# Decoder layer, feed-forward part: the quantiser works on centred values, and the deviation moves into the output scale

## What is computed

```
def layer_norm(x):                      # EPS = 1e-6, Q_B = 128
    return (x - mean(x)) / sqrt(var(x) + EPS)
def absmax_quant(x):
    gamma = max(abs(x)); return clip(x * Q_B / gamma, -Q_B + EPS, Q_B - EPS) * gamma / Q_B
def bitlinear(x, w):
    return absmax_quant(layer_norm(x)) @ ternary(w).T * mean(abs(w))
h = gelu(bitlinear(layernorm(x), w_fc))        # 512 -> 2048, per row of x
x = x + bitlinear(h, w_proj)                   # 2048 -> 512
```

## Time and profile before

| | us |
|---|---|
| median of 3 runs (1135.46 to 1136.88) | 1136.7 |
| the profiled execution | 1134.52 |
| its span, first to last instruction | 1132.7 |

### The profile page before, as it was taken

How to read it: one execution, slowest core, us unless ns; L and a number is a source line. 1 busy time by engine, 2 the same in 40 slices (tenths; PEclk the granted TensorE clock), 3 DMA queues, 4 the chain that set the end, 5 groups by cost and what they waited for, 6 DMA issues and landing times. The chain is left out here.

```text
span 1132.7 us, 18945 instructions
## 1 busy us (share of the span) xinstructions
PE 1003.6 (89%) x6034; PEld 760.6 (67%) x6034; DVE 958.9 (85%) x1351; ACT 793.3 (70%) x1529; POOL 625.1 (55%) x509
## 2 busy tenths in 40 slices
PE   7998988999988999789899985887888998989997
PEld 5555666669664668556567664676767776878886
DVE  5758898996998869998986789899999999998654
ACT  4656756765786776888767696827988978984432
POOL 1369485554536796456738831569655655544401
PEclk9999999999988999899999986997899999989999
DMA  5325356364435545323555460420111110000000
GB/s 194 114 76 171 109 151 184 105 198 152 116 103 182 154 131 168 103 81 106 167 190 159 139 194 6 175 105 26 41 47 34 38 33 32 26 16 19 10 19 19
DMA packets 59360, 115.91 MB, mean 102 GB/s; under 512 B 8880, under 2 KB 13232, under 8 KB 58240
## 3 DMA queue, kind: packets, MB, share of 16 engines
q1 hardware_dynamic: 59264, 114.70, 32.4%
HBM read 90.42 MB, written 24.25 MB: 101 GB/s over the span
## 5 line engine op out<-in xcount | busy, mean ns | idle before, releaser
L1248 POOL TENSOR_TENSOR hb<-du,b_bc 128x1024 f32<-128x1024 f32 (+1 forms) x160 | 314.8, 1987 | 160.6 <-PE ps L1708 160.6
L1795 DVE TENSOR_TENSOR_SCAN hb<-ps,hb 128x1024 f32<-128x1024 f32 (+1 forms) x128 | 257.4, 2013 | 33.3 <-ACT ps L1377 20.0
L1377 ACT ACTIVATE ps<-delta,a_neg 128x511 f32<-128x511 f32 (+2 forms) x320 | 180.6, 600 | 79.5 <-DVE hb L1795 73.3
L1817 DVE SCALAR_TENSOR_TENSOR y_acc<-ps,ct,y_acc 128x512 f32<-128x512 f32 x256 | 181.2, 740 | 24.5 <-PE ps L1708 23.8
L1708 PE MATMUL ps<-ident,hb 128*128 128x128 f32 x1088 | 160.1, 288 | 43.8 <-DVE hb L1795 12.7
L1708 PEld LDWEIGHTS ps<-ident,hb 128*128 128x128 f32 x1088 | 127.8, 147 | 72.1 <-issue 14.2
L1487 ACT ACTIVATE p_q<-ps,m_col 128x512 f32<-128x512 f32 (+3 forms) x256 | 131.5, 530 | 20.9 <-DVE m_col L1892 12.2
L1639 PE MATMUL ps<-xn_t,w_ring 128*128 128x512 f32 x256 | 117.9, 604 | 0.8 <-DVE o_t L1908 0.6
L1766 PE MATMUL ps<-t_fc,xq_hi 128*128 128x512 f32 x256 | 106.2, 415 | 3.2 <-DVE hq_lo L2007 3.2
L1682 PE MATMUL ps<-ident,p_q 128*128 128x128 f32 x640 | 91.9, 287 | 14.4 <-ACT p_q L1487 7.2
L1503 ACT ACTIVATE p_t<-ps 128x512 f32<-128x512 f32 x160 | 88.2, 605 | 22.9 <-PE ps L1682 22.6
(11 more groups left out here) (151 smaller groups left out, 2016.5 us busy)
## 6 DMA issues: line engine op xcount, KB each, us to landing
w_ring<-in_w_attn SPq DMA_DIRECT2D x32, 512.0 KB, 3.7
qk_d<-hl SPq DMA_DIRECT2D x64, 256.0 KB
q_st<-qk_d SPq DMA_DIRECT2D x128, 128.0 KB, 2.8
b_bc<-bc_d SPq DMA_DIRECT2D x48, 256.0 KB, 3.9
k_st<-qk_d SPq DMA_DIRECT2D x64, 128.0 KB, 2.7
k_st<-qk_d SPq DMA_DIRECT2D x128, 64.0 KB, 2.3
x_in<-in_x SPq DMA_DIRECT2D x16, 256.0 KB, 2.9
raw_fc<-in_w_fc SPq DMA_DIRECT2D x4, 1024.0 KB, 9.2
```

The costliest lines, as they stand in the source:

```text
L1248: nc.gpsimd.tensor_tensor(piece_of(e, hi, lo).rearrange("p (a n) -> p a n", a=2), du[b % 2][:, 2 * h:2 * h + 2, lo:hi], b_bc[:, i % BC_RIN ...
L1377: ins = nc.scalar.activation(factors(j, hi, lo)[:, (hi - lo) * m + start:(hi - lo) * (m + 1)], delta[b % 2][:, et, lo + start:hi], ACT.Exp ...
L1795: v.tensor_tensor_scan(h, d, h, 0.0, ALU.mult, ALU.add).then_inc(scan_done, 1)
L1817: v.scalar_tensor_tensor(out=y, in0=bank(kind, r, tb), scalar=ct[:, b % 2, tb, n:n + 1], in1=y, op0=ALU.mult, op1=ALU.add).then_inc(y_free ...
```

## The change

Both quantisers now work on the centred row, without the division by the deviation. In xc, DVE subtracts the mean only. In hn, ACT computes mean - h (scale -1 as a constant, bias the mean), and the minus sign is put right in the output scale. The 1/deviation that POOL computes goes into the scale: for xc it is multiplied in beside the weights' mean, for hscale it is made ahead, with the minus sign, by hstat's last instruction. The number of instructions and their shapes stay; the DVE's xc no longer waits for POOL's xa, and ACT's hn no longer for POOL's hstat, but POOL's own scale steps do. Since the 4 slots of the small buffers could now be overwritten early, DVE's BN_AGGR waits for POOL's work on the tile four before. The due times stay as they are.

```
@@ follows
     elif kind == "xc":
-        yield "dve", 1.9, [pool("xa", t), pe("xt", t - 2) if t >= 2 else dve("wo", B - 1, 1, 1)]
-        yield "pool", 1.5, [dve(*item), dve("wtot", 0)] + ([act("fc", t - 4, 3)] if t >= 4 else [])
+        yield "dve", 1.9, [dve("xa", t), pe("xt", t - 2) if t >= 2 else dve("wo", B - 1, 1, 1)]
+        yield "pool", 1.5, [dve(*item), pool("xa", t), dve("wtot", 0)] + ([act("fc", t - 4, 3)] if t >= 4 else [])
...
     elif kind == "hstat":
-        yield "dve", 0.35, [dve("fc", *a, 3)]
-        yield "pool", 1.1, [dve(*item)]
+        yield "dve", 0.35, [dve("fc", *a, 3)] + ([pool("hstat", a[0] - 4)] if a[0] >= 4 else [])
+        yield "pool", 1.1, [dve(*item), dve("wtot", 1)]
     elif kind == "hn":
-        yield "act", 1.3, [pool("hstat", a[0])]
+        yield "act", 1.3, [dve("hstat", a[0])]
...
     elif kind == "hscale":
-        yield "pool", 0.3, [dve(*item), dve("wtot", 1)]
+        yield "pool", 0.3, [dve(*item), pool("hstat", *a)]
@@ POOL, xc
-                    nc.gpsimd.tensor_scalar(f[:, 12:13], f[:, 8:9], gam[:, 0:1], None, ALU.mult).then_inc(fx_scale, 1)
+                    pool.wait_ge(fx_gain, t + 1)
+                    nc.gpsimd.tensor_scalar(f[:, 12:13], f[:, 8:9], f[:, 7:8], gam[:, 0:1], ALU.mult, ALU.mult).then_inc(fx_scale, 1)
@@ POOL, hstat
-                    nc.gpsimd.tensor_scalar(f[:, 3:4], f[:, 0:1], f[:, 2:3], -1.0, ALU.mult, ALU.mult).then_inc(fh_nmr, 1)
+                    pool.wait_ge(gam_ready, 2)
+                    nc.gpsimd.tensor_scalar(f[:, 3:4], f[:, 2:3], gam[:, 1:2], -1.0, ALU.mult, ALU.mult).then_inc(fh_gain, 1)
@@ POOL, hscale
-                    pool.wait_ge(gam_ready, 2)
-                    nc.gpsimd.tensor_scalar(f[:, 12:13], f[:, 8:9], gam[:, 1:2], None, ALU.mult).then_inc(fh_scale, 1)
+                    pool.wait_ge(fh_gain, t + 1)
+                    nc.gpsimd.tensor_scalar(f[:, 12:13], f[:, 8:9], f[:, 3:4], None, ALU.mult).then_inc(fh_scale, 1)
@@ ACT, hn
-                    act.wait_ge(fh_nmr, t + 1)
+                    act.wait_ge(fh_var, t + 1)
-                    nc.scalar.activation(half, half, ACT.Identity, bias=fh[:, t % 4, 3:4],
-                                         scale=fh[:, t % 4, 2:3]).then_inc(hn_done, 1)
+                    nc.scalar.activation(half, half, ACT.Identity, bias=fh[:, t % 4, 0:1], scale=-1.0).then_inc(hn_done, 1)
@@ DVE, xa and xc
+                    if t >= 4:
+                        dve.wait_ge(fx_gain, t - 3)
                     v.bn_aggr(f[:, 0:2], st_x[:, t % 2]).then_inc(fx_var, 1)
...
-                    dve.wait_ge(fx_pow, t + 1)
...
+                    dve.wait_ge(fx_var, t + 1)
-                    own.done(v.tensor_scalar(x, x2(t), f[:, 0:1], f[:, 7:8], ALU.subtract, ALU.mult))
+                    own.done(v.tensor_scalar(x, x2(t), f[:, 0:1], None, ALU.subtract))
@@ DVE, hstat
+                    if t >= 4:
+                        dve.wait_ge(fh_gain, t - 3)
                     v.bn_aggr(f[:, 0:2], st_h[:, t % 2]).then_inc(fh_var, 1)
```

More of the change, by code:

```diff
@@ L973, in layer_kernel @@
         fx_var = sem("fx_var")
-        fx_pow = sem("fx_pow")
+        fx_gain = sem("fx_gain")
         fx_max = sem("fx_max")
@@ L985, in layer_kernel @@
         fh_scale = sem("fh_scale")
-        fh_nmr = sem("fh_nmr")
+        fh_gain = sem("fh_gain")
         hn_done = sem("hn_done")
@@ L1318, in _ @@
                     own.settle()
-                    nc.gpsimd.tensor_scalar(f[:, 7:8], f[:, 2:3], f[:, 3:4], None, ALU.mult).then_inc(fx_pow, 1)
+                    nc.gpsimd.tensor_scalar(f[:, 7:8], f[:, 2:3], f[:, 3:4], None, ALU.mult).then_inc(fx_gain, 1)
                 elif kind == "xc":
```

## The result

| | before | after |
|---|---|---|
| median of the runs, us | 1136.43 (6 runs, 1135.26 to 1136.88) | 1140.39 (6 runs, 1138.35 to 1140.84) |
| ratio, 95% interval | 1 | 1.0033 (1.002 to 1.0046) |
| profiled execution, us | 1134.52, span 1132.7 | 1140.38, span 1138.5 |
| scan 96 starts at, us | 730.99 | 734.68 |
| from scan 96 to SyncE's closing drain, us | 401.5 | 403.6 |

The time lies in the range (1129.5 to 1140.5) but on the other side of before, where rival B had put it. The last two rows serve all that follows. Scan n is the n-th of the 160 pieces into which DVE's scan is cut, and the feed-forward tiles run beside scans 96 to 159; SyncE's closing drain stands 0.2 us ahead of the end of the span. Up to scan 96 every kernel here runs the same instructions in the same order, yet that part ended between 729.6 and 736.5 us from one profiled execution to another.

The account below looks back on a forecast made before the run. DVE was taken to set the pace up to tile 9's quantiser, PE behind it; -2.93 + 1.0 - 0.66 - 0.2 + 1.85 - 0.55 - 1.35 = -2.84 gave 1133.9 us against the median 1136.7, range 1129.5 to 1140.5.

Parts of the forecast that it names:

- rival B: Second block behind the transposes makes gelu late; DVE waits up to 1.86 us at tiles 6 to 9: 1140.3 us; chance 0.24.
- the first of the three pieces of the forecast: Time of tile 9's quantiser; the others are PE's work behind it and what PE waits after that.
- DVE's waits taken away, -2.93: Up to tile 9's quantiser, DVE's waits of 0.93, 0.55 and 1.45 us go: -2.93 us.
- rival A: No change: DVE is full, waits removed before 1007 are made elsewhere, new ones the full 2.9 us: 1135.8 us; chance 0.23.
- New waits, +1.0, with 2.9 as the upper end: On DVE the new order brings its own waits, between none and all removed (0 to 2.9 us): +1.0 us.
- -0.66 for tile 8's output: In DVE's queue the output of tile 8 now stands behind tile 9's quantiser: -0.66 us.
- Pointer, -0.2: DVE's xc reads one scalar per partition less, 0 to 0.8 us over 13 tiles: -0.2 us.
- ACT's pass to 1150: ACT's normalising pass loses a scale operand from memory and goes from 1236 to about 1150 ns.
- Table loads, 0: Three more ACT table loads at 1283 ns put 0 on the path; without cover 3.85 us.
- PE's deferred block, +1.85: On PE, tile 10's second block now stands behind tile 9's transposes, with no later gap to absorb it: +1.85 us.
- Fillers, -0.55: In the full PE stretch, five fillers ahead of tile 13's transposes go: -0.55 us.
- Last chain, -1.35: Near the end, tile 14's chain loses POOL's step, so PE's wait for its quantised row shortens: -1.35 us.

Follow-up runs that it names:

- The run with tile 10's block ahead: Changed kernel with tile 10's second feed-forward block ahead of tile 9's transposes again, on PE and for ACT's gelu: 1139.69 us, ratio 1.0014 to before.
- the clean pair: Changed kernel with tile 10's second block moved ahead of tile 9's transposes, and the same with tile 11's ahead of tile 10's too: 1139.69 and 1135.28 us.
- the run with the dependency from tile 2 on: Changed kernel's instructions, with the planner seeing the shortened dependency only from tile 2 on: 1133.44 us, ratio 0.9979 to before.
- The joined run without them: Changed instructions, new and old order joined at a scan, which one unstated; new first, joined at 120, 128, 144, 152: 1129.55, 1130.67, 1135.73, 1133.59 us.
- POOL's item: Changed kernel with POOL's gain chain of tile 10 back behind its inputs to scans 144 and 145: 1137.85 us, ratio 1.0012 to before.
- the order joined at scan 128: Changed kernel's instructions, in its new order up to scan 128 and the order of before behind it: 1130.67 us, ratio 0.9956 to before.
- the run with 0.59: Changed kernel with tile 11's second feed-forward block ahead of tile 10's transposes again: 1137.37 us, ratio 0.9998 to before.
- the run with the gate additions moved: Changed kernel with two gate additions put ahead of tile 5's third-block statistics and tile 8's search on DVE: 1137.10 us, ratio 0.9999 to before.

## Why the prediction was wrong

Almost all of the miss lies ahead of tile 9's quantiser, the first of the three pieces of the forecast. From scan 96 to its start (the TENSOR_SCALAR on h_sb) it is 275.96 us before, 275.33 with the edit alone (the changed instructions in the order of before) and 278.18 in the changed kernel: 2.2 later, where the sum had it 2.8 earlier (-2.93 + 1.0 - 0.66 - 0.2). Behind it the changed kernel takes 0.2 us less than before, and the sum had 0.05 less (+1.85 - 0.55 - 1.35). By its own steps:

- *DVE's waits taken away, -2.93.* The wait of 0.55 went: tile 9's quantiser is 0.6 us earlier there. The wait of 0.93 at 819.96 did not go (1.42 in that run). It had never been POOL's. ACT's rows of before show what the chain of one row back had hidden:

```profile
816.81 1.28 ACT L1546 ACT_TABLE_LOAD   x1
818.11 0.69 ACT L1546 ACTIVATE h_sb<-ps,fx 128x512 f32<-128x512 f32 x1
818.69 1.23 ACT L1565 ACTIVATE h_sb<-h_sb,fh 128x1024 f32<-128x1024 f32 x1
```

  The pass begins the moment that the gelu ahead of it in ACT's own list lets it: no [idle <-POOL]. And the 1.45 for the projection, which I counted as gone because the output was put elsewhere, became 2.78. In all, DVE's waits up to tile 9's quantiser (those over 0.15 us) are 6.7 us before and 8.1 with the edit alone, while its work there fell by 1.8 us: it came to the others' products sooner. So the argument against rival A, that the same order can only wait less, doesn't hold for DVE.
- *New waits, +1.0, with 2.9 as the upper end.* **This step failed.** DVE's waits up to tile 9's quantiser are 10.3 us in the changed kernel, 3.5 more than before, where I had 1.9 less (-2.93 + 1.0). And the new order, which was to bring that quantiser 1.1 us forward (-1.45 for the projection's wait, -0.66 for tile 8's output, +1.0), puts it 2.85 us back (278.18 for 275.33). I bounded new waits by those removed, and nothing ties the one to the other. The largest has a second price that I left out, the clock after the idle time. Behind the handover it goes on: to tile 11's quantiser DVE spends 315.65 us on 466 instructions, as many as before in 313.09, and the changed ones in the order of before take 309.99. So the new order costs 5.7 us up to there, 2.85 to tile 9's quantiser, 1.0 to tile 10's and 1.8 to tile 11's, and the last is the deferred block below.
- *-0.66 for tile 8's output* is inside the 2.85 us and can't be told apart.
- *Pointer, -0.2.* xc went from 639 to 505 ns with the order of before, 1.6 us in twelve, yet scan 152 came at the same time (+0.03): nothing on the path up to there. The 214 against 154 of the earlier trace rows was too little to go by.
- *ACT's pass to 1150.* 1141 ns. Right.
- *Table loads, 0.* Ninety-nine for ninety-six. A load is 1.28 us and the next activation starts 1.30 us after it began (816.81, 818.11 above). The Trainium skill's "ScalarE: Activation LUTs", section "What ACT_TABLE_LOAD costs", would have it 2.66; no such drain shows here. But the sign that I named for the loads did come. They stand in the chain that ended last, for 20.2 us behind scan 96 (17.4 in before's), five of them between 925.5 and 937.8, ahead of tile 6's first search for the maximum, where before's chain has PE and POOL:

```profile
927.56 1.28 ACT L1360
...
929.75 1.28 ACT L1548
```

  The run with tile 10's block ahead has two loads fewer and gains nothing by it. No run takes the loads away at tiles 6 to 8 alone, so that they cost nothing isn't shown; they are a rival for the part of the loss that has no name.
- *PE's deferred block, +1.85.* 1.7 by the clean pair, and 1.7 again for the run with the dependency from tile 2 on (-2.0 for -3.7). I gave it to tile 10's block behind tile 9's transposes; it is tile 11's behind tile 10's, where I had said that nothing is added. The size came out right by luck: one block is as long as another. The handover had moved one tile on (PE idles 1.27 us ahead of tile 10's transposes, before not at all), which was one of my signs of being wrong.
- *Fillers, -0.55.* The joined run without them gains 0.54 there. Right.
- *Last chain, -1.35.* 1.40 in that run, and in all that have the new chain. The rows after (the earlier trace rows before): joined mean 1105.23 + 0.26, pass from 1105.53, and PE no longer waits.

```profile
1105.23 0.26 DVE L2022 BATCH_NORM_AGGREGATE fh<-st_h 128x2 f32<-128x24 f32 x1
1106.72 1.22 DVE L2027 TENSOR_REDUCE fh<-h_sb 128x1 f32<-128x1024 f32 x1 [1.22 <-ACT h_sb L1567]
1105.53 1.15 ACT L1567 ACTIVATE h_sb<-h_sb,fh 128x1024 f32<-128x1024 f32 x1 [1.06 <-DVE fh L2022]
```

- *Not in the sum:* in the order of before PE idles 3.76 us ahead of tile 9's transposes instead of 4.38 and is at the higher clock earlier: 2.28 us from the y product at 1015.19 to the next for 3.38 before. That made the projection of tile 9 1.35 us earlier. So the edit alone gains 0.6 + 1.35 + 0.3 + 1.4 = 3.7 us, the 0.3 between the projections of tiles 9 and 10.

Rival B had the right sign by the wrong place, and its 1140.3 met the measured 1140.4 by luck. Waits for late gelu do show, but ahead of tile 9's quantiser there is one of 1.53 us (1005.36) in place of B's four of 1.86, and 1.12 and 0.82 come at tile 11; moving tile 10's block gave nothing. The costs that could be shown are tile 11's block and the idle time with its clock at tile 4. Where the rest of the 5.7 us sits stays open, POOL's item and the table loads among the candidates; in the traces a wait mended at one place came back in part at the next.

## What to carry to other kernels

Where a planner reads what you edit, time the two apart: the new instructions in the old order first. Here that is a gain of 0.3%, and 0.56% with the early part of the new order, which the plain edit turns into a loss of 0.33%. Due times fitted to one outcome are no model: a change of 0.05 us in an estimate moved the time by 0.9%, so no new order should be priced by what it was meant to save. And before a wait is called removed, look two steps back: what was the engine that is waited for waiting for itself?

## What the hardware showed that I had not expected

After an idle time of 3.15 us PE had the lower clock level for the next 5.6 us, which cost 2.6 us more in matmuls; after one of 1.55 us at the same place (two executions) it cost none. The low level came in all nine executions that have 3.15 or 3.16 us directly ahead of this projection, for 9.3 to 10.4 us. But the length of the idle time alone doesn't tell: behind 2.75 us (old instructions, new order) it took 7.7, and behind 1.75 us, with transposes between, 7.7 in the order of before and 9.3 in the order joined at scan 128. Identical instruction streams are not identical in time: a wait of 0 or 1.16 us at about 929 us, one of 1.53 or 0.59 at 1004, and 7 us of spread in the first 731 us come and go between executions. At 929 it is PE's clock, low or high behind the same 2.72 us of idle time. At 1004 the clock isn't all: eight transposes behind 2.58 us of idle time took 1.97 us in the changed kernel, with a wait of 1.53, and 1.09 in the run with 0.59, but 1.09 also with 1.53 in the run with the gate additions moved. So a loss of 1 us read from a single pair of traces is no finding unless the waits ahead of it agree.
